# The y products of an AdaLN-conditioned FFN with LoRA experts: two 64-row products per batch pair in place of one block-diagonal product of 128 rows

## The chip, the cores and the metric

The kernel runs on one core of a Trainium2 chip. The metric is the device time of one execution in microseconds (us), as the median of several runs; lower is better. TensorE does the matrix products, ScalarE (ACT), VectorE (DVE) and GpSimd (POOL) copy, split and sum, and SyncE (SP) issues nearly all DMAs.

## The reference, cut to what matters

```python
y = einsum('bct,bcd->bdt', x, W[cond])                 # per batch b: a 64 x 64 matrix, x[b] is 64 x 1024
base = einsum('bsi,oi->bso', y, W_org)                 # 1024 x 1024 projection
q = einsum('bi,ki->bk', y.mean(axis=1), Wq)
coeffs = softmax(einsum('bk,ek->be', q, lora_keys) / sqrt(128))
h = einsum('bsi,eir->bser', y, lora_down)              # 8 experts of rank 64, so 512 columns
out = x + base + einsum('be,bser,ero->bso', coeffs, h, lora_up)
```

There are 64 batches of 64 rows and 1024 columns, all in fp32. The change touches only the first line, which makes y.

## The kernel before

**Tiles.** Two batches make a tile: `x_sb[:, i, :]` has the 64 rows c of batch 0 on partitions 0 to 63 and those of batch 1 on 64 to 127, 1024 columns each. There are 32 tiles, t = 0 to 31, and four tiles make a group q, of which there are 8. x is the stationary operand (what is loaded into TensorE's array), 128 columns at a time, and `cws` is the moving one: a 128 x 128 block diagonal of the two batches' 64 x 64 matrices, copied out of `table` into a buffer whose off-diagonal blocks are set to zero once. One matmul thus gives 128 columns of x by (batch, d) for both batches. A tile takes 8 such matmuls, in two halves n = 2t and 2t + 1 of 4 matmuls each (`make_y(n)`); a half fills one PSUM bank of 512 fp32 columns. An fp32 matmul of the program shows in the trace as two weight loads and two matmuls, so a tile's y is 16 of each. The matmuls of the rest take operands of type fp32r and show as one load and one matmul each.

**After y.** ScalarE copies each half to `y_full` (`copy_y`), from which it is stored to DRAM and summed for the gate, and y is split for the products that follow into a high and a low part, `yq_h` and `yq_l` (`split_y`). Of the first four tiles the even halves are split straight from PSUM, ScalarE making the high part and VectorE the low part and the copy. `make_h(q, a, r)` multiplies the split y of a group by `down` (three passes of high and low parts); then come the LoRA `up` products, and after 380 us the base projection (line 1473), which makes no y.

**Order.** All orders are written out by hand, engine by engine, with semaphores between them. On TensorE a group is: `make_h` quarter, y of one tile of the next group, `make_h` quarter, y of the next tile, and so on four times, then the `up` products. Six of the first eight halves (0, 1, 2, 4, 6, 3; the table `FIRST`) come before the first `make_h`, number 5 within it and number 7 behind it. Twelve matmuls on zeros (line 1520) and the transposition of the LoRA keys (line 1523) stand at the very start; `make_gate` (line 1407) multiplies the keys by `Wq` once. `y_ps`, `h_ps`, `x_ps` and `w_ps` are pairs of PSUM banks. In the steady state the halves of y take turns between the two banks of `y_ps`, and half n waits until half n - 2 has been copied out (`copied(n - 2)`). `y_done` counts finished halves.

Of the kernel before, what the change touches and what calls it, by code (L numbers as in the profile page):

```python
# [26 lines left out]
def adaln_ffn(  # L27
# [51 lines left out]
    with ExitStack() as ctx:  # L79
# [201 lines left out]

        FIRST = (0, 1, 2, 4, 6, 3, 5, 7)
        BY_DVE = (0, 2, 4, 6)
        BY_ACT = (1, 3, 5, 7)

        BEFORE = {6: 0, 3: 1, 5: 2, 7: 4, 8: 6, 9: 3}

        def made(n):
            return FIRST.index(n) + 1 if n < 8 else n + 1

        def tile_made(t):
            return max(made(2 * t), made(2 * t + 1))

# [232 lines left out]
        def _(pool):  # L526
# [10 lines left out]
            def turn_cw(t, rows):  # L537

                if t >= 3:
                    pool.wait_ge(y_done, tile_made(t - 3))  # L540
                for b in range(BT):

                    pool.wait_ge(cw_ready, cw_count(t) + b)
                    pool.tensor_copy(cws[b * C:(b + 1) * C, t % 3, b:b + 1, :, :], table_of(rows[b])).then_inc(cw_ready, 1)  # L544

# [23 lines left out]
            rows_1 = rows_of(1)  # L569
            pool.wait_ge(first_steps, 4)  # L570
            pool.wait_ge(table_loaded, 16)
# [31 lines left out]
        def _(act):  # L603
            def copy(dst, src, done):
                nc.scalar.activation(dst, src, ACT.Copy).then_inc(done, 1)  # L605
# [5 lines left out]
            def turn_cw(t, rows):  # L611
                for b in range(BT):
                    copy(cws[b * C:(b + 1) * C, t % 3, b:b + 1, :, :], table_of(rows[b]), cw_by_act)

            def copy_y(n):
                t, r = n // 2, n % 2
                act.wait_ge(y_done, made(n))
                if n >= 8:

                    act.wait_ge(y_summed, max(n - 7, 8))  # L620
                    act.wait_ge(y_lo[r], t - 3)
                    act.wait_ge(y_stored[n % 8], 16 * (n // 8))
                copy(y_full[:, n % 8, :, :], y_bank(n).rearrange("p (k n) -> p k n", k=4), y_copied)

            def split_y(n):
                t, r = n // 2, n % 2
                i = t % 4
                if n in BY_DVE:

                    act.wait_ge(y_done, made(n))  # L630
                    copy(yq[0][:, 0:4, i * P:(i + 1) * P], y_bank(n).rearrange("p (k n) -> p k n", k=4), y_hi[0])
# [88 lines left out]
            act.dma_start(keys_sb[:, :], lora_keys).then_inc(keys_loaded, 16)  # L720
            act.wait_ge(first_steps, 4)

# [5 lines left out]
            turn_cw(2, rows_2)  # L728
            split_y(0)

            act.wait_ge(y_done, tile_made(0))
            turn_cw(3, rows_3)
            copy_y(1)
            split_y(2)
            split_y(4)
            split_y(6)
            split_down_half(0, 0)
            split_down_half(1, 0)
            split_y(1)
            copy_y(3)  # L740
            split_y(3)
            copy_y(5)
            split_down_half(0, 1)
            split_down_half(1, 1)
            split_y(5)
            copy_y(7)
            split_y(7)
# [126 lines left out]
        def _(dve):  # L874
# [6 lines left out]
            def copy_y(n):  # L881

                dve.wait_ge(y_hi[0], BY_DVE.index(n) + 1)
                nc.vector.tensor_copy(y_full[:, n % 8, :, :],
                                      y_bank(n).rearrange("p (k n) -> p k n", k=4)).then_inc(y_copied_dve, 1)

# [9 lines left out]
            def split_y(n):  # L896
                t, r = n // 2, n % 2
                i = t % 4
                dve.wait_ge(y_hi[r], t + 1)
                if n in BY_DVE:  # L900

                    sub(yq[1][:, 0:4, i * P:(i + 1) * P], y_bank(n).rearrange("p (k n) -> p k n", k=4),
                        yq[0][:, 0:4, i * P:(i + 1) * P], y_lo[0])
# [244 lines left out]
            copy_y(0)  # L1148
            split_y(2)
            split_y(4)  # L1150
            split_y(6)
            split_down_half(0, 0)
            copy_y(2)
            split_down_half(1, 0)
            copy_y(4)
            copy_y(6)
# [180 lines left out]
        def _(pe):  # L1337
            def make_y(n):
                t, r = n // 2, n % 2
                i = t % 4  # L1340
                pe.wait_ge(x_loaded[i], 16 * (t // 4 + 1))
                if n == 1:
# [14 lines left out]
                mm.then_inc(y_done, 1)  # L1357

            def make_h(q, a, r):

                bank = (x_ps, h_ps)[a]
                pe.wait_ge(y_hi[r], 4 * q + 4)
                if q > 0 or a > 0 or r > 0:
                    pe.wait_ge(y_lo[r], 4 * q + 4)
# [5 lines left out]
                for m in range(2):  # L1370
# [10 lines left out]
                    if q == 0 and a == 0 and r == 0 and m == 0:  # L1381

                        for i, (s, w) in enumerate(PASSES):
                            if i == 1:
                                pe.wait_ge(y_lo[0], 4)
                            elif i == 2:
                                pe.wait_ge(down_lo[0], 1)
                            for k in range(4):
                                nc.tensor.matmul(bank[:, m, :], down[w][:, k, col:col + P], yq[s][:, k, :],
                                                 start=(k == 0 and i == 0), stop=False, skip_group_check=True)  # L1390
                        make_y(5)
                        continue
# [10 lines left out]
            def make_gate():  # L1403
                pe.wait_ge(keys_ready, 1)
                pe.wait_ge(wq_loaded, 16)
                for k in range(KC):
# [112 lines left out]
            for n in range(12):  # L1519
                nc.tensor.matmul(w_ps[:, 0, 0:P], gs[:, 0, 0, :], gs[:, 0, 0, :], start=True, stop=True)  # L1520
            pe.wait_ge(first_steps, 4)
            pe.wait_ge(keys_loaded, 16)
            nc.tensor.transpose(keys_ps, keys_sb[:, :], ident[0:E, 0:E]).then_inc(keys_turned, 1)
            for n in FIRST[:6]:
                make_y(n)
            for q in range(NQ):
# [3 lines left out]
                for a in range(2):  # L1530
                    for r in range(2):
                        m = 2 * a + r
                        make_h(q, a, r)
                        if m == 0 and q == 0:
                            make_y(7)
                            make_gate()
                        if m == 1:
                            make_scores(q)
                        if more:
                            make_y(n + 2 * m)  # L1540
                            make_y(n + 2 * m + 1)
                up_1(j0)
# [53 lines left out]
```

## Time and profile before

| | before |
|---|---|
| median of 3 runs | 710.55 us (710.32 to 710.64) |
| the profiled execution | 710.81 us, span of its instructions 709.0 us |
| TensorE matmul busy | 700.6 us (99%) |
| TensorE weight loads busy | 587.1 us (83%) |
| VectorE / ScalarE / GpSimd busy | 504.0 / 287.4 / 127.0 us |

The span runs from the first to the last instruction; 1.8 us of the execution's time lie outside it. Weight loads (PEld) are a row of their own, since they overlap the matmuls (PE). A matmul's duration runs to when its last result is out, so that matmuls that follow closely overlap in the records; what a series of them costs is read from the starts.

### The profile page before, as it was taken

The page shows a single profiled execution, that of the slowest core. Times are in us where ns is not written, and L with a number is a line of the kernel's source. Part 1 is how long each engine was busy: PE and PEld are TensorE (multiplying, and loading weights), DVE is VectorE, ACT ScalarE, POOL GpSimd, SP SyncE. Part 2 cuts the span into 40 slices and gives each one's busy share as a digit, 9 for nine tenths or more (in the row PEclk, how much of TensorE's full clock was granted, in tenths as well). Part 3 has the DMA queues.
Part 4 walks back from the last instruction along what each step waited for, and adds up shares of the span by engine and source line. Part 5 has one row for each costly group of instructions (what it writes and reads, how often), then busy time and mean ns, then how long its engine had stood idle before and what let it go on. Part 6 is the DMA issues. An engine that isn't in the chain of part 4 may idle for free.

```text
span 709.0 us, 10597 instructions
## 1 busy us (share of the span) xinstructions
PE 700.6 (99%) x3345; PEld 587.1 (83%) x3345; DVE 504.0 (71%) x821; ACT 287.4 (41%) x584; POOL 127.0 (18%) x136
## 2 busy tenths in 40 slices
PE   8999999999999999999999999999999999999997
PEld 7887878888888888888888878888888888888876
DVE  4998596685765874655756997668767677776774
ACT  4566666855757642532624722222112222221220
POOL 3310000100100000000000043232332333323360
PEclk9999999999999999999999999999999999999999
DMA  8993393673853934432444836666667776766732
GB/s 240 317 347 125 101 307 137 189 227 128 248 189 120 281 120 120 137 129 62 149 149 146 337 122 188 218 217 217 223 215 238 237 238 223 237 206 213 272 113 89
DMA packets 97049, 137.80 MB, mean 194 GB/s; under 512 B 14810, under 2 KB 66018, under 8 KB 94178
## 3 DMA queue, kind: packets, MB, share of 16 engines
q1 hardware_dynamic: 96976, 137.12, 59.6%
q8 instruction: 27, 0.44, 0.2%
q14 instruction: 28, 0.23, 0.1%
q10 hardware_dynamic: 18, 0.00, 0.0%
HBM read 81.53 MB, written 55.57 MB: 193 GB/s over the span
## 4 chain that ended last, share of the span: by engine, by line
PE 83%; DVE 7%; issue 4%; DMA 2%; SPq 2%; ACT 2%; DVEq 0%; ACTq 0%
PE x_ps L1473 23%; PE w_ps L1473 17%; PE x_ps L1429 11%; PE h_ps L1395 9%; PE x_ps L1395 9%; PE w_ps L1429 8%; PE y_ps L1354 5%; DMA up_raw<-in_L_ffn_lora_up_dram 1%; DMA x_sb<-in_x_dram 1%; SPq L340 1%; DVE ysum L892 1%; DVE tu_l L876 1%; DVE tb_l L876 1%; ACT st L605 1%; DVE blk L879 1%
## 5 line engine op out<-in xcount | busy, mean ns | idle before, releaser
L558 POOL TENSOR_TENSOR blk<-blk,blkx 128x512 f32<-128x512 f32 x60 | 94.1, 1570 | 274.9 <-DVE blk L879 204.7
L879 DVE TENSOR_TENSOR blk<-w_ps,blk 128x512 f32<-128x512 f32 x96 | 66.1, 688 | 67.0 <-PE w_ps L1429 31.0
L1473 PE MATMUL x_ps<-tb_h,ba_h 128*128 128x512 f32 x256 | 100.0, 391 | 0.8 <-DVE ba_l L876 0.4
L1473 PE MATMUL x_ps<-tb_l,ba_h 128*128 128x512 f32 x256 | 99.6, 389 | 0.0
L1473 PE MATMUL x_ps<-tb_h,ba_l 128*128 128x512 f32 x256 | 99.6, 389 | 0.0
L605 ACT ACTIVATE ba_h<-bs 128x512 fp32r<-128x512 f32 x64 | 38.1, 625 | 124.6 <-DVE bs L876 124.6
L1473 PE MATMUL w_ps<-tb_h,ba_h 128*128 128x512 f32 x192 | 74.9, 390 | 0.0
L1473 PE MATMUL w_ps<-tb_l,ba_h 128*128 128x512 f32 x192 | 74.7, 389 | 0.0
L1473 PE MATMUL w_ps<-tb_h,ba_l 128*128 128x512 f32 x192 | 74.7, 389 | 0.0
L544 POOL COPY cws<-table 64x64 f32 x60 | 20.3, 338 | 287.1 <-PE y_ps L1354 274.9
L605 ACT ACTIVATE ba_h<-yb 128x512 fp32r<-128x512 f32 x48 | 28.4, 621 | 103.1 <-DMA yb<-y_dram 103.1
L879 DVE TENSOR_TENSOR blk<-x_ps,blk 128x512 f32<-128x512 f32 x64 | 42.5, 683 | 34.3 <-PE x_ps L1473 34.3
L605 ACT ACTIVATE st<-wt 32x256 f32<-32x256 f32 x128 | 53.1, 415 | 19.4 <-DVE wt L1055 16.5
L1354 PEld LDWEIGHTS y_ps<-cws,x_sb 128*128 128x128 f32 x480 | 57.4, 191 | 3.1 <-issue 0.9
L1354 PE MATMUL y_ps<-cws,x_sb 128*128 128x128 f32 x480 | 59.0, 276 | 0.8 <-ACT y_full L605 0.4
L892 DVE TENSOR_REDUCE ysum<-y_full 128x8 f32<-128x512 f32 x64 | 40.8, 678 | 26.4 <-ACT y_full L605 26.4
L605 ACT ACTIVATE blk<-x_ps 128x512 f32<-128x512 f32 x64 | 38.3, 598 | 51.8 <-PE x_ps L1429 49.7
L876 DVE TENSOR_TENSOR ba_l<-bs,ba_h 128x512 fp32r<-128x512 f32 x64 | 59.2, 944 | 0.0
L1473 PEld LDWEIGHTS x_ps<-tb_h,ba_h 128*128 128x128 f32 x256 | 48.0, 188 | 12.2 <-issue 1.3
L1473 PEld LDWEIGHTS x_ps<-tb_l,ba_h 128*128 128x128 f32 x256 | 48.0, 188 | 10.0
L1473 PEld LDWEIGHTS x_ps<-tb_h,ba_l 128*128 128x128 f32 x256 | 48.1, 188 | 9.9
L1395 PE MATMUL h_ps<-yq_h,down_h 128*128 128x512 f32 x128 | 51.1, 399 | 0.0
(103 smaller groups left out, 1406.2 us busy)
## 6 DMA issues: line engine op xcount, KB each, us to landing
y_dram<-y_full SPq DMA_DIRECT2D x64, 256.0 KB, 3.7
yb<-y_dram SPq DMA_DIRECT2D x32, 512.0 KB, 7.2
out_dram<-blk SPq DMA_DIRECT2D x64, 256.0 KB, 3.9
x_sb<-in_x_dram SPq DMA_DIRECT2D x31, 512.0 KB, 5.3
blkx<-in_x_dram SPq DMA_DIRECT2D x30, 512.0 KB, 7.0
r_dram<-blk SPq DMA_DIRECT2D x56, 256.0 KB, 2.4
blk<-r_dram SPq DMA_DIRECT2D x14, 1024.0 KB, 6.6
t_dram<-st SPq DMA_DIRECT2D x16, 448.0 KB, 5.2
```

Source lines behind the costliest of these rows:

```text
L340: sp.dma_start(raw_piece(n).rearrange("p a k r -> p (a k) r"), down_v[n]).then_inc(down_loaded[n], 16)
L544: pool.tensor_copy(cws[b * C:(b + 1) * C, t % 3, b:b + 1, :, :], table_of(rows[b])).then_inc(cw_ready, 1)
L558: pool.tensor_tensor(blk[p % 3][:, b, :], blk[p % 3][:, b, :], blkx[:, h, n, :], ALU.add).then_inc(x_added, 1)
L605: nc.scalar.activation(dst, src, ACT.Copy).then_inc(done, 1)
L876: nc.vector.tensor_tensor(dst, a, b, ALU.subtract).then_inc(done, 1)
L879: nc.vector.tensor_tensor(dst, a, b, ALU.add).then_inc(done, 1)
L892: nc.vector.tensor_reduce(ysum[:, 4 * r:4 * r + 4, BT * (t % 4):BT * (t % 4) + BT], y_full[:, n % 8, :, :].rearrange("p k (b d) -> p k b d ...
L1354: mm = nc.tensor.matmul(y_bank(n)[:, k * P:(k + 1) * P], x_sb[:, i, col:col + P], cws[:, t % 3, :, :, :].rearrange("p b h d -> p (b h d)") ...
L1395: mm = nc.tensor.matmul(bank[:, m, :], down[w][:, k, col:col + P], yq[s][:, k, :], start=(k == 0 and i == 0), stop=(k == KC - 1 and i == 2 ...
L1429: mm = nc.tensor.matmul(bank, ga[s][:, n, e, :], tu[w][:, n, e, :], start=(first and e == 0 and i == 0), stop=(e == 1 and i == 2), skip_gr ...
L1473: mm = nc.tensor.matmul(bank, ba[s][n][:, k, :], tb[w][n][:, k, :], start=(first and k == 0 and i == 0), stop=(k == 3 and i == 2), skip_gr ...
```

## The change

Each batch of a tile now has matmuls of its own: 64 rows of x are loaded (partitions 0 to 63 for batch 0, 64 to 127 for batch 1) and 64 columns of that batch's own 64 x 64 matrix are streamed. A tile is 16 matmuls of the program instead of 8, in the order k = 0 batch 0, k = 0 batch 1, k = 1 batch 0 and so on. Batch b writes bank b of a pair of banks, so a tile fills a pair, and a half n (k 0 to 3 or 4 to 7) lies in both banks. `cws` has no zero blocks any more, so it is half as wide and its memset is gone. The first three tiles lie in `y_ps`, `w_ps`, `h_ps`, then `y_ps`, `w_ps`, and from tile 5 on all in `y_ps`; a tile waits until both halves of the tile before it in its banks are copied out. All four tiles of the first group are made before the first `make_h`. Since ScalarE and VectorE now read the same banks, waits keep their copies apart in the first four tiles.

```diff
-        cws = small("cws", [P, 3, BT, 2, C // 2])
+        cws = small("cws", [P, 3, 2, C // 2])
-        keys_ps = h_ps[:, 0, 0:E]
+        keys_ps = x_ps[:, 0, 0:E]
...
-        def y_bank(n):
-
-            if n < 8:
-                return (y_ps, w_ps)[n in (2, 4, 5, 7)][:, n not in (0, 6, 2, 5), :]
-            return y_ps[:, n % 2, :]
+        def y_banks(t):
+
+            return (y_ps, w_ps, h_ps, y_ps, w_ps)[t] if t < 5 else y_ps
+
+        def tile_before(t):
+
+            return t - 3 if t < 5 else (t - 2 if t < 6 else t - 1)
+
+        def y_half(n):
+
+            t, r = n // 2, n % 2
+            return y_banks(t)[:, :, 4 * r * C:4 * (r + 1) * C].rearrange("p b (k d) -> p b k d", d=C)
...
-            pool.memset(cws[:, :, :, :, :], 0.0).then_inc(first_steps, 1)
...
             def copy_y(n):
                 t, r = n // 2, n % 2
-                act.wait_ge(y_done, made(n))
+                act.wait_ge(y_done, tile_made(t))
...
-                copy(y_full[:, n % 8, :, :], y_bank(n).rearrange("p (k n) -> p k n", k=4), y_copied)
+                if n == BY_ACT[-1]:
+
+                    act.wait_ge(y_copied_dve, len(BY_DVE))
+                copy(by_batch(y_full[:, n % 8, :, :]), y_half(n), y_copied)
...
-            def make_y(n):
-                t, r = n // 2, n % 2
+            def make_y(t):
...
-                if n in BEFORE:
-                    pe.wait_ge(*copied(BEFORE[n]))
-                elif n >= 10:
-                    pe.wait_ge(*copied(n - 2))
-                for k in range(4):
-                    col = (4 * r + k) * P
-                    mm = nc.tensor.matmul(y_bank(n)[:, k * P:(k + 1) * P], x_sb[:, i, col:col + P],
-                                          cws[:, t % 3, :, :, :].rearrange("p b h d -> p (b h d)"),
-                                          start=True, stop=True)
-                mm.then_inc(y_done, 1)
+                if t >= 3:
+                    for r in range(2):
+                        pe.wait_ge(*copied(2 * tile_before(t) + r))
+                for k in range(KC):
+                    for b in range(BT):
+                        rows64 = slice(b * C, (b + 1) * C)
+                        mm = nc.tensor.matmul(y_banks(t)[:, b, k * C:(k + 1) * C], x_sb[rows64, i, k * P:(k + 1) * P],
+                                              cws[rows64, t % 3, :, :].rearrange("p h d -> p (h d)"),
+                                              start=True, stop=True)
+                        if k == KC - 1:
+                            mm.then_inc(y_done, 1)
```

This is TensorE's program from its first y product to its first h product, of before (`x3` behind a row is three more of the same; `128x128` is the output):

```order
L1354 MATMUL y_ps<-cws,x_sb 128x128 [waits cw_ready,x_loaded_0]
L1354 MATMUL y_ps<-cws,x_sb 128x128 x3
L1354 MATMUL y_ps<-cws,x_sb 128x128 [waits cw_ready,x_rest_loaded,x_loaded_0]
L1354 MATMUL y_ps<-cws,x_sb 128x128 x3
L1354 MATMUL w_ps<-cws,x_sb 128x128 [waits cw_ready,x_loaded_1]
L1354 MATMUL w_ps<-cws,x_sb 128x128 x3
L1354 MATMUL w_ps<-cws,x_sb 128x128 [waits cw_by_act,x_loaded_2]
L1354 MATMUL w_ps<-cws,x_sb 128x128 x3
L1354 MATMUL y_ps<-cws,x_sb 128x128 [waits y_copied_dve,cw_by_act,x_loaded_3]
L1354 MATMUL y_ps<-cws,x_sb 128x128 x3
L1354 MATMUL y_ps<-cws,x_sb 128x128 [waits y_copied,cw_ready,x_loaded_1]
L1354 MATMUL y_ps<-cws,x_sb 128x128 x3
```

And the same stretch of the changed kernel:

```order
L1365 MATMUL y_ps<-cws,x_sb 128x64 [waits cw_ready,x_rest_loaded,x_loaded_0]
L1365 MATMUL y_ps<-cws,x_sb 128x64 x15
L1365 MATMUL w_ps<-cws,x_sb 128x64 [waits cw_ready,x_loaded_1]
L1365 MATMUL w_ps<-cws,x_sb 128x64 x15
L1365 MATMUL h_ps<-cws,x_sb 128x64 [waits cw_by_act,x_loaded_2]
L1365 MATMUL h_ps<-cws,x_sb 128x64 x15
L1365 MATMUL y_ps<-cws,x_sb 128x64 [waits y_copied_dve,y_copied,cw_by_act,x_loaded_3]
L1365 MATMUL y_ps<-cws,x_sb 128x64 x15
L1408 MATMUL x_ps<-yq_h,down_h 128x512 [waits c12_ready,down_hi,keys_ready,y_hi_0]
```

Six half tiles of 4 matmuls became four whole tiles of 16 smaller ones; the halves that stood within and behind the first h products are among them.

Further on, a tile between two h quarters, TensorE before:

```order
L1354 MATMUL y_ps<-cws,x_sb 128x128 [waits y_copied,cw_ready,x_loaded_2]
L1354 MATMUL y_ps<-cws,x_sb 128x128 x3
L1354 MATMUL y_ps<-cws,x_sb 128x128 [waits y_copied,cw_ready,x_loaded_2]
L1354 MATMUL y_ps<-cws,x_sb 128x128 x3
```

and in the changed kernel (two rows of tile 6, then the `up` products behind tile 7):

```order
L1365 MATMUL y_ps<-cws,x_sb 128x64 [waits y_copied,cw_ready,x_loaded_2]
L1365 MATMUL y_ps<-cws,x_sb 128x64 x15
...
L1365 MATMUL y_ps<-cws,x_sb 128x64 [waits y_copied,cw_ready,x_loaded_3]
L1365 MATMUL y_ps<-cws,x_sb 128x64 x15
L1450 MATMUL x_ps<-tu_h,ga_h 128x512 [waits tu_hi,tu_lo,ga_lo_0,ga_hi_0]
```

The place in the order is the same; the number of matmuls doubles, and the one wait covers both halves of the tile before.

## Rows read from the trace of the kernel before

**Rows 1.** Page: busy us, share of the span, instructions of each engine; granted TensorE clock.

```profile
PE 700.6 (99%) x3345; PEld 587.1 (83%) x3345; DVE 504.0 (71%) x821; ACT 287.4 (41%) x584; POOL 127.0 (18%) x136
...
PEclk9999999999999999999999999999999999999999
```

**Rows 2.** Page: the chain of work that ended last, by engine.

```profile
PE 83%; DVE 7%; issue 4%; DMA 2%; SPq 2%; ACT 2%; DVEq 0%; ACTq 0%
```

**Rows 3.** Busy us by stage, instructions in brackets, granted clock, DMA share, GB/s.

```profile
0.00:34.00 34.00, 31.82 (x194) 28.66 (x195) 23.10 (x39) 15.65 (x29) 12.64 (x26) 1.00 0.96 275
34.00:380.00 346.00, 344.24 (x1728) 291.66 (x1727) 236.88 (x464) 190.68 (x417) 14.37 (x46) 1.00 0.53 169
380.00:709.00 329.00, 324.55 (x1426) 266.74 (x1424) 244.04 (x320) 81.02 (x139) 99.98 (x64) 1.00 0.64 213
```

**Rows 4.** The same stages, the y products (line 1354) alone.

```profile
0.00:34.00 34.00, 12.53 (x96) 11.48 (x96) 1.00 0.96 275
34.00:380.00 346.00, 50.91 (x416) 49.95 (x416) 1.00 0.53 169
```

**Rows 5.** Waits of TensorE, 34 to 380 us: us in total, times, longest.

```profile
PE w_ps L1429 <- DVE ga_l L876: 1.0, 1, 1.0
PE y_ps L1354 <- ACT y_full L605: 0.4, 1, 0.4
```

**Rows 6.** Timeline of TensorE around a tile's y: start us, us, work.

```profile
225.67 0.22 PE L1418 MATMUL h_ps<-zs,ones_r 128*128 128x128 f32 x1
225.73 2.00 PE L1354 MATMUL y_ps<-cws,x_sb 128*128 128x128 f32 x16
227.48 0.48 PE L1395 MATMUL h_ps<-yq_h,down_h 128*128 128x512 f32 x1
```

**Rows 7.** Timeline of TensorE's weight loads, same stretch.

```profile
225.67 1.86 PEld L1354 LDWEIGHTS y_ps<-cws,x_sb 128*128 128x128 f32 x16
227.45 0.19 PEld L1395 LDWEIGHTS h_ps<-yq_h,down_h 128*128 128x128 f32 x1
```

**Rows 8.** Lines 1407 and 1523: duration ns min/median/max, first and last start us.

```profile
L1407 PEld LDWEIGHTS h_ps<-keys_t,wq_raw x16: 192/192/192, 21.2 to 22.8; 128*128 128x128 f32 x16
L1407 PE MATMUL h_ps<-keys_t,wq_raw x16: 175/256/256, 21.3 to 22.9; 128*128 128x8 f32 x16
...
L1523 PEld LDWEIGHTS h_ps<-ident,keys_sb x1: 135/135/135, 6.2 to 6.2; 8*128 8x128 f32 x1
```


**Rows 9.** Timeline of weight loads, 5.8 to 6.75 us.

```profile
5.49 0.55 PEld L1520 LDWEIGHTS w_ps<-gs 128*128 128x128 f32 x3
6.16 0.14 PEld L1523 LDWEIGHTS h_ps<-ident,keys_sb 8*128 8x128 f32 x1
6.59 0.30 PEld L1354 LDWEIGHTS y_ps<-cws,x_sb 128*128 128x128 f32 x2 [0.30 <-issue]
```

**Rows 10.** Timeline of weight loads at the gate products.

```profile
21.16 1.87 PEld L1407 LDWEIGHTS h_ps<-keys_t,wq_raw 128*128 128x128 f32 x16
22.94 1.87 PEld L1354 LDWEIGHTS y_ps<-cws,x_sb 128*128 128x128 f32 x16
```

**Rows 11.** Timeline of ScalarE and of TensorE around 80 us.

```profile
79.31 1.08 ACT L605 ACTIVATE y_full<-y_ps 128x512 f32<-128x512 f32 x2
...
80.05 2.02 PE L1354 MATMUL y_ps<-cws,x_sb 128*128 128x128 f32 x16 [0.35 <-ACT y_full L605]
```

**Rows 12.** Timeline of TensorE, start of the program.

```profile
11.45 2.05 PE L1354 MATMUL y_ps<-cws,x_sb 128*128 128x128 f32 x16 [0.20 <-DMA x_sb<-in_x_dram]
13.91 1.17 PE L1389 MATMUL x_ps<-yq_h,down_h 128*128 128x512 f32 x4 [0.40 <-ACT down_h L605]
...
16.75 1.05 PE L1354 MATMUL w_ps<-cws,x_sb 128*128 128x128 f32 x8
```

**Rows 13.** Timeline of GpSimd, start of the program.

```profile
0.73 0.42 POOL L561 MEMSET cws<- 128x384 f32 x1 [0.29 <-POOLq L1585]
...
5.85 0.23 POOL L544 COPY cws<-table 64x64 f32 x1 [4.02 <-DMA table<-in_L_cond_weights_dram]
```

More of the change, by code:

```diff
@@ L278, in b_sum @@
             return bs[n][:, :, :].rearrange("p k (a d) -> p k a d", a=4)
-        FIRST = (0, 1, 2, 4, 6, 3, 5, 7)
         BY_DVE = (0, 2, 4, 6)
         BY_ACT = (1, 3, 5, 7)
-        BEFORE = {6: 0, 3: 1, 5: 2, 7: 4, 8: 6, 9: 3}
-        def made(n):
-            return FIRST.index(n) + 1 if n < 8 else n + 1
         def tile_made(t):
-            return max(made(2 * t), made(2 * t + 1))
+            return 2 * t + 2
         def cw_count(t):
@@ L306, in copied, with by_batch @@
             return y_copied, BY_ACT.index(n) + 1
-        def y_bank(n):
-            if n < 8:
-                return (y_ps, w_ps)[n in (2, 4, 5, 7)][:, n not in (0, 6, 2, 5), :]
-            return y_ps[:, n % 2, :]
+        def y_banks(t):
[5 more added lines that the diff above has]
+            return y_banks(t)[:, :, 4 * r * C:4 * (r + 1) * C].rearrange("p b (k d) -> p b k d", d=C)
+        def by_batch(half):
+            return half.rearrange("p k (b d) -> p b k d", b=BT)
         def down_half(s, n, r):
@@ L543, in turn_cw @@
                     pool.wait_ge(cw_ready, cw_count(t) + b)
-                    pool.tensor_copy(cws[b * C:(b + 1) * C, t % 3, b:b + 1, :, :], table_of(rows[b])).then_inc(cw_ready, 1)
+                    pool.tensor_copy(cws[b * C:(b + 1) * C, t % 3:t % 3 + 1, :, :], table_of(rows[b])).then_inc(cw_ready, 1)
             def add_xz(b):
@@ L569, in _ @@
             rows_1 = rows_of(1)
-            pool.wait_ge(first_steps, 4)
+            pool.wait_ge(first_steps, 3)
             pool.wait_ge(table_loaded, 16)
@@ L612, in turn_cw @@
                 for b in range(BT):
-                    copy(cws[b * C:(b + 1) * C, t % 3, b:b + 1, :, :], table_of(rows[b]), cw_by_act)
+                    copy(cws[b * C:(b + 1) * C, t % 3:t % 3 + 1, :, :], table_of(rows[b]), cw_by_act)
             def copy_y(n):
                 t, r = n // 2, n % 2
-                act.wait_ge(y_done, made(n))
+                act.wait_ge(y_done, tile_made(t))
                 if n >= 8:
@@ L628, in split_y @@
                 if n in BY_DVE:
-                    act.wait_ge(y_done, made(n))
-                    copy(yq[0][:, 0:4, i * P:(i + 1) * P], y_bank(n).rearrange("p (k n) -> p k n", k=4), y_hi[0])
+                    act.wait_ge(y_done, tile_made(t))
+                    copy(by_batch(yq[0][:, 0:4, i * P:(i + 1) * P]), y_half(n), y_hi[0])
                     return
@@ L720, in _ @@
             act.dma_start(keys_sb[:, :], lora_keys).then_inc(keys_loaded, 16)
-            act.wait_ge(first_steps, 4)
+            act.wait_ge(first_steps, 3)
             copy(sexp[:, 0, :], ident[:, 0:E], act_ready)
@@ L729, in _ @@
             split_y(0)
-            act.wait_ge(y_done, tile_made(0))
+            copy_y(1)
             turn_cw(3, rows_3)
-            copy_y(1)
             split_y(2)
+            copy_y(3)
             split_y(4)
+            copy_y(5)
             split_y(6)
@@ L739, in _ @@
             split_y(1)
-            copy_y(3)
             split_y(3)
-            copy_y(5)
+            copy_y(7)
             split_down_half(0, 1)
@@ L745, in _ @@
             split_y(5)
-            copy_y(7)
             split_y(7)
@@ L883, in copy_y @@
                 dve.wait_ge(y_hi[0], BY_DVE.index(n) + 1)
-                nc.vector.tensor_copy(y_full[:, n % 8, :, :],
-                                      y_bank(n).rearrange("p (k n) -> p k n", k=4)).then_inc(y_copied_dve, 1)
+                if n < BY_DVE[-1]:
+                    dve.wait_ge(*copied(n + 1))
+                nc.vector.tensor_copy(by_batch(y_full[:, n % 8, :, :]), y_half(n)).then_inc(y_copied_dve, 1)
             def sum_y(n):
@@ L900, in split_y @@
                 if n in BY_DVE:
-                    sub(yq[1][:, 0:4, i * P:(i + 1) * P], y_bank(n).rearrange("p (k n) -> p k n", k=4),
-                        yq[0][:, 0:4, i * P:(i + 1) * P], y_lo[0])
+                    if n < BY_DVE[-1]:
+                        dve.wait_ge(*copied(n + 1))
+                    sub(by_batch(yq[1][:, 0:4, i * P:(i + 1) * P]), y_half(n),
+                        by_batch(yq[0][:, 0:4, i * P:(i + 1) * P]), y_lo[0])
                     return
@@ L1149, in _ @@
             split_y(2)
+            copy_y(2)
             split_y(4)
@@ L1152, in _ @@
             split_down_half(0, 0)
-            copy_y(2)
+            copy_y(4)
             split_down_half(1, 0)
-            copy_y(4)
             copy_y(6)
@@ L1337, in _ @@
         def _(pe):
-            def make_y(n):
-                t, r = n // 2, n % 2
+            def make_y(t):
                 i = t % 4
                 pe.wait_ge(x_loaded[i], 16 * (t // 4 + 1))
-                if n == 1:
+                if t == 0:
                     pe.wait_ge(x_rest_loaded, 16)
@@ L1362, in make_h @@
                 pe.wait_ge(y_hi[r], 4 * q + 4)
+                if q == 0 and a == 0 and r == 0:
+                    pe.wait_ge(keys_ready, 1)
+                if q == 0 and a == 1 and r == 0:
+                    for n in (4, 5):
+                        pe.wait_ge(*copied(n))
                 if q > 0 or a > 0 or r > 0:
@@ L1405, in make_gate @@
                 pe.wait_ge(wq_loaded, 16)
+                for n in (4, 5):
+                    pe.wait_ge(*copied(n))
                 for k in range(KC):
@@ L1520, in _ @@
                 nc.tensor.matmul(w_ps[:, 0, 0:P], gs[:, 0, 0, :], gs[:, 0, 0, :], start=True, stop=True)
-            pe.wait_ge(first_steps, 4)
+            pe.wait_ge(first_steps, 3)
             pe.wait_ge(keys_loaded, 16)
             nc.tensor.transpose(keys_ps, keys_sb[:, :], ident[0:E, 0:E]).then_inc(keys_turned, 1)
-            for n in FIRST[:6]:
-                make_y(n)
+            for t in range(4):
+                make_y(t)
             for q in range(NQ):
@@ L1534, in _ @@
                         if m == 0 and q == 0:
-                            make_y(7)
                             make_gate()
@@ L1539, in _ @@
                         if more:
-                            make_y(n + 2 * m)
-                            make_y(n + 2 * m + 1)
+                            make_y(4 * (q + 1) + m)
                 up_1(j0)
```

1 line of the change is left out of this document (removed).

## The prediction

> **What bounds the kernel now.** The page's first part and the chain of waits say it together: TensorE's matmuls are busy in 700.6 us of 709.0, at the full granted clock all along [rows 1], and 83% of the chain that ended last is TensorE [rows 2]. The stretches tell where y lies: 344.2 of the 346 us between 34 and 380 us are busy, and y is 416 of the 1728 matmul records there, with 96 more before 34 us; behind 380 us, where the base projection runs, there is none [rows 3, 4]. TensorE's waits in that middle stretch come to under 2 us [rows 5]. So whatever a tile's y costs on TensorE, more or less, arrives in the time nearly in full, and what the other engines do matters only where it makes TensorE wait.
>
> What does one tile's y cost, and what in it is the limit? The busy figure (275 ns or so a record) can't say it, since records overlap. The starts can. The weight loads of a tile begin at 225.67 us and the next h load at 227.45 [rows 7]: 1.78 us for 16 loads, 0.111 us each. 32 tiles make 57.0 us. Whether loading or streaming sets the 0.111 is told by the gate products. They load 128 columns too but stream only 8 columns instead of 128, and their 16 loads take from 21.16 to 22.94 us, 0.111 each again [rows 8, 10]. With next to nothing to stream the step is the same, so **y is bound by its weight loads**, and the matmuls lie beside them. This decides the reading of the change: it halves what is streamed, which costs nothing now, and doubles the number of loads.
>
> **The change part by part.**
>
> *The loads.* A tile's 8 program matmuls become 16, so 16 loads become 32, each of 128 columns but 64 rows; 512 loads are added over the 32 tiles. No row has a 64-row load. The bounds are these.
> - If loads of the two batches go one after the other at the price of a full one: 512 x 0.111 = +57.0 us.
> - If a load of batch 1 runs wholly beside one of batch 0, since they fill different rows of the array: each half of the array gets the 16 loads per tile that the whole array gets now, and the sum is 0.
> - If loads overlap and a 64-row load is also cheaper, the sum is negative. The row nearest to it is the keys' load of 8 rows: 135 ns against the gate loads' 192 [rows 8]. The 57 ns less, taken off the step of 0.111, leave 0.054; half the price and full overlap would be 256 x (0.111 - 0.2225) = -28.5 us, counting by the 256 pairs of k and tile, each of which costs two steps, 0.2225, now. I don't take this one, since that row is a transposition, which differs in more than its rows (it shows one load, where fp32 products of the program show two).
>
> Between the ends I take overlap with a lag. A program matmul of fp32 is load, matmul, load, matmul, and then comes the other batch. The second load of a batch needs the first one's place free, a full step later; the first load of the next batch stands behind that batch's second matmul in the queue and can follow about 0.03 us later (a load at 227.45 us, its matmul at 227.48 [rows 6, 7]), and then runs beside it. A round of both batches is so 2 x (0.111 + 0.030) = 0.282 us against 0.2225, +0.060 for each of 256: **+15.3 us**. If the matmul of 64 columns has to be streamed first (half of 0.111, 0.056, as a bound, since 128 columns take no longer than the step), it is 2 x (0.111 + 0.056) = 0.334, or +28.5.
>
> The Trainium skill, page "TensorE: Matmul & The Clock Gate", section "LDWEIGHTS (loading the stationary operand)", gives the time of a load as columns over 1.2 GHz and says that a load of 32 rows takes what one of 128 rows takes. For 128 columns that is an estimate of 107 ns, beside the measured 111; it speaks against this change, for by it no load becomes cheaper, and the best sum is 0. The 135 ns of the 8-row load don't fit it, unless the transposition explains them.
>
> *Going in and out of half-array products.* The keys' matmul is the one place where the rows in use change. Its load starts at 6.16 us; the last load of the zeros before it starts at 5.49 + 0.55 - 0.19 = 5.85 us [rows 8, 9]. That is 0.31 us where 0.111 is usual: 0.20 us more, which may be a wait for the array to empty or for a semaphore. The y of tiles 4 to 31 stand singly between h products and the first four together, so there are 29 stretches. I price the way in at 0.20 (+5.8 us) and leave the way out at nothing, because the matmul before it is short; bounds are 0 and both ways, +11.6 us.
>
> The Trainium skill, page "TensorEngine Tiling (Array Packing)", section "Key Properties", says that changing the tiling mode drains TensorE, and that different tiles can load weights and multiply in parallel. By the first the 5.8 us are real; by the second the overlap is, though whether two loads run together it doesn't say, and no run of this trace shows it.
>
> *Waits.* A tile now waits for both halves of the tile before it, whose second copy used to be wanted only half a tile later. Tile 9 already waits (start at 80.05 us, 0.35 us idle), and ScalarE's two copies run from 79.31 to 80.39 us [rows 11]: +0.4 us, once, since the other waits for y copies don't exist [rows 5]. Behind the waiting y stands only the next h quarter, and a delay there is in the sum already. Copies start up to 0.9 us later, as they want a whole tile; ScalarE is busy in 190.7 of 346 us [rows 3], and the copies that nothing else follows on TensorE for a quarter of h have that as cover; without it each tile would cost up to 0.9 us. That copies read 64-column runs out of two banks instead of one run of 512 I price at nothing under the same cover.
>
> *The start.* Before, six halves are done and the first h product starts at 13.91 us, with y halves put in at 16.75 and later. Now eight halves come first. The last tile of before starts at 11.45 us, held by its DMA [rows 12]; three whole tiles from 6.59 us [rows 9] end at 6.59 + 5.3 = 11.9 at today's price. The first h product comes some 1.8 us later, two halves (1.8 us) are gone from behind it, sum 0 but for the price of y, which is counted above. The memset of `cws` takes 0.42 us from 0.73 us on, and GpSimd then idles 4.02 us for the table [rows 13]; dropping it gives 0.
>
> **Sum.** 710.81 + 15.3 + 5.8 + 0.4 = 732.3 us for the profiled execution. That one lies 0.26 over the median of the runs, so 732 us for the median.
>
> **The rivals.**
> - *Loads in series.* The two batches' loads don't run together, at 0.111 each: 710.5 + 57.0 + 5.8 + 0.4 = 773.7, from 768 without to 780 with both switches. For it: loads follow one another at the same step wherever the trace has several, whatever is streamed. Against it: all of those use the whole array, so they could not overlap. Chance 0.30.
> - *A 64-row load costs half, and loads overlap* (faster than before). For it: 135 ns against 192. From 710.5 - 28.5 + 5.8 = 688 to, with the lag of 0.030, 256 x (2 x (0.054 + 0.030) - 0.2225) = -14, 702. It decides once a round of both batches with its share of the switches (5.8 / 256 = 0.023) is under 0.2225, that is once a load costs less than 0.070 with that lag. Chance 0.22.
> - *Nothing changes*: full overlap, no lag, switches that cost under 1.4 us. Or the loads are half price and in series, with free switches. 710 to 712. Chance 0.08.
>
> **How the numbers follow.** The forecast, overlap with lag, has 0.40; its own range is from 712 (no lag, little for the switches) to 710.5 + 28.5 + 11.6 + 0.4 = 751. The range has to reach to the serial case, or it would leave out 3 in 10, and takes in no change: 700 to 778, which leaves out most of the faster case and the last end of the serial one. Below 0.2% (1.4 us) this kernel's measurement can't tell a change from none. Faster 0.22, no change 0.08, slower 0.40 + 0.30 = 0.70.
>
> **What would show it.** In the changed profile the loads of a tile's y, 32 of them, should take 2.26 us plus the switch from the first to the next h load; 3.6 us means series, 1.8 full overlap, under 1.4 cheaper loads. The gap between the last h load and the first y load shows the switch: 0.2 us more than today's. The chain of waits should remain TensorE's, with no new wait of over 1 us for copies. I am wrong in sign if the y stretch is shorter than 1.78 us, and wrong in mechanism if the time grows by idle time of TensorE on ScalarE's copies.

## The result, and the profile after

The changed kernel takes 724.35 us (median of 4 runs, 721.95 to 728.62) against 710.43 for the kernel before: a ratio of 1.0202, 95% interval 1.0177 to 1.0228. It is slower, by 13.9 us, inside the predicted range and 8 us under the forecast. The profiled execution took 726.1 us. The spread of 6.7 us is itself news, since the kernel before spreads by 1 us in its four runs; it goes with the granted clock: the four runs have 0.987, 0.995, 0.986 and 0.994 for 726.1, 721.95, 728.62 and 722.59 us.

The head of the page, to be read against [rows 1, 2]: TensorE is 99% busy as before, and the chain is now 92% TensorE. What is new is the clock, low in slices 1 and 2 of 40.

```profile
span 724.3 us, 11627 instructions
...
PE 716.1 (99%) x3857; PEld 594.3 (82%) x3857; DVE 504.1 (70%) x821; ACT 285.5 (39%) x584; POOL 121.3 (17%) x135
...
PEclk7799999999999999999999999999999999999999
...
PE 92%; DVE 3%; issue 2%; ACT 1%; DMA 1%; DVEq 0%; POOL 0%; SPq 0%; ACTq 0%; POOLq 0%
```

**The y of a tile.** The weight loads of tile 17, of which [rows 7] show the kernel before:

```profile
237.08 0.19 PEld L1439 LDWEIGHTS h_ps<-zs,ones_r 128*128 128x128 f32 x1
237.45 1.86 PEld L1365 LDWEIGHTS y_ps<-cws,x_sb 64*128 64x128 f32 x32 [0.19 <-issue]
239.38 0.19 PEld L1413 LDWEIGHTS h_ps<-yq_h,down_h 128*128 128x128 f32 x1
```

32 loads take 1.86 us, exactly as long as 16 took. A load of 64 rows is about as long as one of 128:

```profile
L1365 PEld LDWEIGHTS y_ps<-cws,x_sb x928: 182/188/330, 7.1 to 353.3; 64*128 64x128 f32 x186
```

The median is 188 ns, where it was 192 for 128 rows. So the two batches' loads run side by side, and pair follows pair at the old step: (1.86 - 0.19) / 15 = 0.111 us. Next, the same tile's matmuls, for [rows 6]:

```profile
237.30 0.22 PE L1439 MATMUL h_ps<-zs,ones_r 128*128 128x128 f32 x1
237.46 2.00 PE L1365 MATMUL y_ps<-cws,x_sb 64*128 64x64 f32 x32
239.39 0.50 PE L1413 MATMUL h_ps<-yq_h,down_h 128*128 128x512 f32 x1
```

From the start of the scores product (the one on `zs`) to the start of y it was 0.06 us and is 0.16; from y to the next h product it was 1.75 and is 1.93. Together 0.28 us are lost here. How they divide between the way in and the way out depends on whether matmuls or loads are read. These are the loads at the way into tile 16, with the last h load before it, in the kernel before and in the changed one:

```profile
217.98 0.19 PEld L1395 LDWEIGHTS x_ps<-yq_h,down_l 128*128 128x128 f32 x1
218.20 1.98 PEld L1354 LDWEIGHTS y_ps<-cws,x_sb 128*128 128x128 f32 x16
...
229.25 0.19 PEld L1413 LDWEIGHTS x_ps<-yq_h,down_l 128*128 128x128 f32 x1
229.79 1.86 PEld L1365 LDWEIGHTS y_ps<-cws,x_sb 64*128 64x128 f32 x32 [0.35 <-issue]
```

The first y load came 0.22 us after the last h load and now comes 0.54 after it, so by the loads nearly all of the loss lies before the stretch. The loads now stand idle before 27 of the y stretches between 34 and 380 us, 8.8 us in all and for nothing that the profile shows, where it was 0.6 us, once. Only the sum of both sides is certain. Over a whole group of four tiles it is more accurate. These are the y starts of tiles 16 and 20 of the changed kernel,

```profile
229.79 2.00 PE L1365 MATMUL y_ps<-cws,x_sb 64*128 64x64 f32 x32
...
279.29 2.00 PE L1365 MATMUL y_ps<-cws,x_sb 64*128 64x64 f32 x32
```

and of tiles 4, 16 and 20 of the kernel before:

```profile
22.97 2.03 PE L1354 MATMUL y_ps<-cws,x_sb 128*128 128x128 f32 x16
...
218.43 1.95 PE L1354 MATMUL y_ps<-cws,x_sb 128*128 128x128 f32 x16
...
266.56 1.95 PE L1354 MATMUL y_ps<-cws,x_sb 128*128 128x128 f32 x16
```

A group takes 279.29 - 229.79 = 49.50 us against 266.56 - 218.43 = 48.13: 1.37 more for four tiles, **0.34 us a stretch**. For 28 stretches that is 9.6 us.

**The start** (TensorE's timeline, for [rows 12]) has the rest:

```profile
7.14 2.00 PE L1365 MATMUL y_ps<-cws,x_sb 64*128 64x64 f32 x32 [0.65 <-POOL cws L550]
8.94 3.25 PE L1365 MATMUL w_ps<-cws,x_sb 64*128 64x64 f32 x32
11.93 3.68 PE L1365 MATMUL h_ps<-cws,x_sb 64*128 64x64 f32 x32
15.34 3.68 PE L1365 MATMUL y_ps<-cws,x_sb 64*128 64x64 f32 x32
20.32 2.05 PE L1408 MATMUL x_ps<-yq_h,down_h 128*128 128x512 f32 x4 [1.29 <-ACT down_h L610]
...
30.55 2.00 PE L1365 MATMUL w_ps<-cws,x_sb 64*128 64x64 f32 x32
```

From the start of the first tile's y to that of the second it is 1.80 us, then 2.99 and 3.41, the fourth tile's record is as long as the third's, and tile 4 starts its y at 30.55 us, where the kernel before had it at 22.97 (the first row of its y starts above). Busy time by stretch says why (the brackets hold numbers of instructions; the first figure behind the last bracket is the granted clock, 1.00 being 2.4 GHz and 0.50 being 1.2):

```profile
5.00:9.00 4.00, 3.35 (x43) 3.17 (x42) 0.17 (x1) 0.51 (x2) 0.93 (x4) 1.00 1.00 352
9.00:26.00 17.00, 15.71 (x112) 14.30 (x110) 9.59 (x14) 8.44 (x18) 3.43 (x4) 0.51 1.08 252
26.00:34.00 8.00, 8.00 (x67) 7.11 (x66) 7.93 (x12) 2.62 (x6) 4.24 (x6) 0.97 1.04 393
```

And the kernel before, from 9 to 26 us:

```profile
9.00:26.00 17.00, 16.23 (x110) 14.48 (x110) 14.78 (x22) 9.80 (x18) 7.25 (x8) 1.00 1.02 245
```

TensorE is nearly as busy as it was, 15.71 of 17 us against 16.23, but at half clock.

The Trainium skill, page "TensorE: Matmul & The Clock Gate", Part 1, says that the clock is set by how busy the engine has been. By these rows an engine that its records show as busy can still get half the clock, and the runs below show what differs.

TensorE's waits in the middle stretch, for [rows 5]:

```profile
PE y_ps L1365 <- ACT y_full L610: 0.4, 1, 0.4
PE x_ps L1450 <- ACT blk L610: 0.3, 1, 0.3
```

No new wait. The wait for the y copy is as long as it was, and the 1.0 us on `ga_l` is gone, presumably because TensorE now comes later to the product that waited for VectorE. Before 34 us there is a longer wait, 1.3 us for `down_h` where it was 0.4 (the 20.32 row above, against [rows 12]).

### The profile page after: what moved, and what is told of

Read it like the earlier page. It is cut to its first block, busy times and chain, and to the rows that moved or that the text cites. A ratio compares the mean times of both kernels' runs of the same rounds, so it can differ in the third digit from the quotient of the medians.

```text
span 724.3 us, 11627 instructions
## 1 busy us (share of the span) xinstructions
PE 716.1 (99%) x3857; PEld 594.3 (82%) x3857; DVE 504.1 (70%) x821; ACT 285.5 (39%) x584; POOL 121.3 (17%) x135
## 4 chain that ended last, share of the span: by engine, by line
PE 92%; DVE 3%; issue 2%; ACT 1%; DMA 1%; DVEq 0%; POOL 0%; SPq 0%; ACTq 0%; POOLq 0%
PE x_ps L1494 22%; PE w_ps L1494 17%; PE h_ps L1413 12%; PE x_ps L1450 11%; PE x_ps L1413 10%; PE w_ps L1450 8%; PE y_ps L1365 8%; DVE tb_l L883 1%; PE x_ps L1408 1%; PE w_ps L1365 1%; DMA table<-in_L_cond_weights_dram 1%; DVE blk L886 1%; DVE ysum L900 0%; PE h_ps L1365 0%; ACT st L610 0%
## 5 line engine op out<-in xcount | busy, mean ns | idle before, releaser
L550 POOL COPY cws<-table 64x64 f32 x60 | 15.0, 250 | 298.8 <-PE y_ps L1365 279.7
L1365 PEld LDWEIGHTS y_ps<-cws,x_sb 64*128 64x128 f32 x928 | 55.8, 192 | 9.5 <-issue 9.5
L1365 PE MATMUL y_ps<-cws,x_sb 64*128 64x64 f32 x928 | 59.7, 280 | 1.1 <-POOL cws L550 0.6
```

The lines of the kernel that those rows point to most:

```text
L550: pool.tensor_copy(cws[b * C:(b + 1) * C, t % 3:t % 3 + 1, :, :], table_of(rows[b])).then_inc(cw_ready, 1)
L1365: mm = nc.tensor.matmul(y_banks(t)[:, b, k * C:(k + 1) * C], x_sb[rows64, i, k * P:(k + 1) * P], cws[rows64, t % 3, :, :].rearrange("p h d ...
```

## The experiments

All times are medians; each is compared with the kernel before on the same chip (710.41 us in the first four, 709.88 in the next four, 709.58 in the last).

**e1, e2: which part of the change costs what.** In e1 tiles 0 to 3 are made as before, in halves of 128 rows in the old order, and only tiles 4 to 31 by the new products. e2 is the reverse.

In `make_y` of e1, on top of the kernel before:

```diff
+                if n >= 8:
+                    if r == 1:
+                        return
+                    for m in ((6, 3) if n == 8 else (n - 2, n - 1)):
+                        pe.wait_ge(*copied(m))
+                    for k in range(KC):
+                        for b in range(BT):
...
```

In `make_y` of e2, on top of the changed kernel (`cws` and its memset are as before the change):

```diff
+                if t >= 4:
+                    for r in range(2):
+                        pe.wait_ge(*copied(2 * tile_before(t) + r))
+                        for k in range(4):
...
```

> The start of the kernel before (block-diagonal halves for tiles 0 to 3), two-batch products of 64 rows from tile 4 on. Theory 1 (the 14 us are the way in and out of half-array products, 0.28 us for each of 28 stretches, plus a lower granted clock near the program's start): 710.4 + 28 x 0.28 = 718 us, clock 1.00 all along, 7.60 us from one tile's y to the next. Rival (the low clock comes with 64-row products wherever they stand): clock below 0.99 again and 724 us. Rival (the loss is all in the start's new order): 710 to 711 us.

Measured: 720.21 us, ratio 1.0140 (1.0124 to 1.0155). The one run at clock 1.000 took 719.52, the three at 0.997 took 720.17 to 720.34. That is 9.1 us for the 28 stretches at full clock, 0.33 each, with nothing taken off for the 1.0 us on `ga_l`, which is gone here too. I expected 718, having read 0.28 off one tile. The clock was not quite full all along as expected: there is a short low stretch, after the first 64-row tile.

```profile
22.00:25.00 3.00, 3.00 (x42) 2.91 (x42) 2.96 (x7) 1.61 (x2) 1.74 (x2) 1.00 1.12 249
25.00:29.00 4.00, 4.00 (x11) 3.11 (x11) 3.94 (x5) 2.16 (x4) 1.94 (x3) 0.57 1.08 354
29.00:33.00 4.00, 4.00 (x31) 3.31 (x29) 2.25 (x6) 0.01 (x1) 0.70 (x2) 1.00 1.00 389
```

> The reverse: the changed kernel's start with four 64-row tiles, block-diagonal halves from tile 4 on. Theory 1: only the start's loss is left, 710.4 + 6 to 7 = 717 us, with a granted clock of 0.98 to 0.99 over the span and a low stretch within the first 30 us. Rival (the start is late because of its order and its waits, with no help of the clock): 717 us as well, but at clock 1.00. Rival (all loss is in the later stretches): 710 us.

Measured: 711.85 us, ratio 1.0043 (1.0021 to 1.0066), from 12 runs. Nine took 711.0 to 712.4 at clock 0.997 to 1.000, three 716.4 to 718.2 at 0.987 to 0.989. The new order of the start costs about 1 us, and the rest is the clock, in some runs only. Where the 1 us arises, the profiled run at full clock shows. Tile 4's y and the h product behind it, in the kernel before and in e2 (both with 128-row products in this tile):

```profile
22.97 2.03 PE L1354 MATMUL y_ps<-cws,x_sb 128*128 128x128 f32 x16
24.76 0.48 PE L1395 MATMUL x_ps<-yq_h,down_h 128*128 128x512 f32 x1
...
23.63 2.03 PE L1368 MATMUL w_ps<-cws,x_sb 128*128 128x128 f32 x16
26.22 0.47 PE L1427 MATMUL x_ps<-yq_h,down_h 128*128 128x512 f32 x1 [0.56 <-POOL yq_l L536]
```

From y to h it was 1.79 us and is 2.59, 0.80 more: the h product now waits for a low part of y that GpSimd writes. e4 and e5 below have the same wait, of 0.5 and 0.6 us. The profiled run of the changed kernel hasn't got it; there TensorE came later, at the low clock, which is presumably why. The expected 717 us was right for three runs of twelve.

**e3: must the batches take turns?** All eight products of batch 0, then those of batch 1.

```diff
-                for k in range(KC):
-                    for b in range(BT):
+                for b in range(BT):
+                    for k in range(KC):
```

> The changed kernel, but batch 0's eight products of a tile first and then batch 1's. If loads run beside each other only when neighbours in the program fill different halves of the array, a tile's 32 loads take 32 x 0.111 = 3.6 us instead of 1.8, and the time is 724 + 32 x 1.8 = 781 us. If the queue reaches far enough to pair them anyway, 724 us and 1.8 us a tile. In between, if some at the seam are paired.

Measured: 804.96 us, one run, clock 0.940. A tile in a stretch at full clock:

```profile
223.25 3.39 PE L1365 MATMUL y_ps<-cws,x_sb 64*128 64x64 f32 x32
226.56 0.50 PE L1413 MATMUL h_ps<-yq_h,down_h 128*128 128x512 f32 x1
```

From y to the next h product it is 3.31 us where it was 1.93, so most loads are in series. Without turns the pairing is gone but for the seam between the batches: from 224.58 to 224.97 us 9 of these loads are under way, and 4 in the same length at the start of the tile (223.25 to 223.64). This is nearly the rival "loads in series". Over 32 tiles the 1.38 us are 44 us, and 720 + 44 = 764. The remaining 41 us I put down to the low clock, which now came back again and again (0.91 in the mean from 34 to 440 us). That is argued, not shown: by the profiled run of the changed kernel, where a mean clock of 0.987 went with 6.3 us over 719.8, a mean of 0.940 over 803 us would be some 32 us, an estimate, which leaves 9 open.

**e4, e5: what brings the clock down.** The products of tiles 0 to 3 (e4) or of all tiles (e5) stream their 64 columns twice, but for the last k of a tile, which streams them once; the second copy lands where the next k is written and is overwritten by it. Loads, rows in use and order stay. This is e5; in e4 `w` is 2 only where also t < 4.

```diff
+                        w = 2 if k < KC - 1 else 1
-                        mm = nc.tensor.matmul(y_banks(t)[:, b, k * C:(k + 1) * C], x_sb[rows64, i, k * P:(k + 1) * P],
-                                              cws[rows64, t % 3, :, :].rearrange("p h d -> p (h d)"),
+                        mm = nc.tensor.matmul(y_banks(t)[:, b, k * C:(k + w) * C], x_sb[rows64, i, k * P:(k + 1) * P],
+                                              cws[rows64, t % 3, :, :].rearrange("p h d -> p (h d)").unsqueeze(1).to_broadcast([C, w, C]),
```

> The changed kernel, but in tiles 0 to 3 each product streams its 64 columns twice (the second copy is overwritten by the next product), so that 128 columns are streamed for each load, as before the change; loads and order stay. If the granted clock falls because the array streams little between the loads, it now stays at full, and the time is 724 - 6 = 718 us. If it falls because only half the rows are in use, or because of waits between the tiles, the start is as in the changed kernel: 722 to 728 us and clock 0.985 to 0.995.

Measured: 722.16 us, ratio 1.0160 (1.0140 to 1.0181): two runs of 718.9 and 719.3 us at clock 0.999, three of 722.2 to 722.5 at 0.995 to 0.998. No run at 0.985 to 0.989 any more, but the median was not the expected 718, so the question stood half open. The weight loads of the start, at twice the columns:

```profile
6.57 1.86 PEld L1366 LDWEIGHTS y_ps<-cws,x_sb 64*128 64x128 f32 x32
8.35 1.87 PEld L1366 LDWEIGHTS w_ps<-cws,x_sb 64*128 64x128 f32 x32
10.13 1.87 PEld L1366 LDWEIGHTS h_ps<-cws,x_sb 64*128 64x128 f32 x32
11.92 1.87 PEld L1366 LDWEIGHTS y_ps<-cws,x_sb 64*128 64x128 f32 x32
```

Each tile's loads start 1.78 us after the last tile's. Streaming 128 columns is free here, as the gate products had said.

> The changed kernel with every y product streaming its 64 columns twice (in the run before, only those of tiles 0 to 3 did). If the low clock comes from how little the array streams per load, no run falls any more: granted clock 0.999 or 1.000 in each, 719 us in each, spread under 1 us. If it comes from the half-array loads themselves, runs of 722 us and clock 0.995 to 0.998 stay. If streaming had a price of its own, the 1.78 us from one tile's first load to the next in the start would grow; I expect it not to.

Measured: 719.87 us, ratio 1.0140 (1.0125 to 1.0156), four runs from 719.53 to 720.32, each at clock 1.000. The same stretches as above:

```profile
5.00:9.00 4.00, 2.79 (x45) 2.60 (x45) 0.17 (x1) 0.75 (x3) 0.92 (x4) 1.00 0.89 344
9.00:26.00 17.00, 15.15 (x167) 13.57 (x164) 14.51 (x21) 9.82 (x19) 7.21 (x8) 1.00 1.11 259
26.00:34.00 8.00, 8.00 (x60) 6.74 (x60) 7.38 (x16) 3.62 (x7) 3.39 (x6) 1.00 1.06 388
```

Streaming more cost nothing: every run lies within 0.6 us of the changed kernel's fastest (719.78 us, below). The array had the same loads, rows and order, and TensorE was no busier from 9 to 26 us (15.15 us against 15.71); only the columns streamed differ, and with them the clock. Four runs would be few to say so, but the three versions below stream the same way: of the 18 runs of e5, e6, e7 and e9, 17 have a clock of 0.999 or 1.000 and one, of e7, 0.997, where 8 of the changed kernel's 10 runs (here and in e8) have 0.985 to 0.997.

**e8: the changed kernel again**, for its runs beside these.

> The changed kernel itself once more, beside the others on one chip: 722 to 728 us with the granted clock going from 0.995 to 0.986 as the time rises; a run at full clock, if there is one, should take 719 us. If runs of one clock differ by more than 1 us, something other than the clock varies.

Measured: 721.01 us, ratio 1.0144 (1.0128 to 1.0159), six runs, four of them below the expected 722: 719.78 and 719.80 us at clock 0.999, 720.84 at 0.997, 721.18 at 0.994, 726.73 at 0.988, 728.00 at 0.985. Time follows the clock. At full clock the change costs 719.8 - 709.9 = 9.9 us, and the low clock adds up to 8.

**e6: is it the stretch or what is in it?** As e5, with the y of tiles 12 to 31 in two stretches.

```diff
+                    if m == 1 and 2 <= q < NQ - 1:
+                        make_y(4 * (q + 1) + 2 * a + r, range(0, 4))
...
-                            make_y(4 * (q + 1) + m)
+                            make_y(4 * (q + 1) + m, range(4, KC) if q >= 2 else range(KC))
```

> As e5, and the y of tiles 12 to 31 is made in two stretches of four k, one in the middle of an h quarter and one behind it, so 20 more stretches. Theory (each stretch of half-array products between whole-array ones costs 0.34 us, whatever its length): e5 + 6.8 us = 726 us. Rival (the price is that of the products in it, a slower step in a stretch, not of going in and out): no more than e5 + 1 us. A third way, waits for copies that now come too soon, would show as TensorE waiting on y_full.

Measured: 728.16 us, ratio 1.0254 (1.0240 to 1.0268), 8.3 us over e5 with the same number of products. TensorE's timeline:

```profile
223.36 0.39 PE L1416 MATMUL x_ps<-yq_h,down_l 128*128 128x512 f32 x1
223.68 1.16 PE L1366 MATMUL y_ps<-cws,x_sb 64*128 64x128 f32 x16
224.77 0.50 PE L1416 MATMUL x_ps<-yq_h,down_h 128*128 128x512 f32 x1
...
227.40 0.39 PE L1416 MATMUL x_ps<-yq_h,down_l 128*128 128x512 f32 x1
227.72 1.11 PE L1366 MATMUL y_ps<-cws,x_sb 64*128 64x128 f32 x16
228.76 0.50 PE L1416 MATMUL x_ps<-yq_h,down_h 128*128 128x512 f32 x1
```

A stretch of half the length has the same edges: 0.32 us from the last h product, where h follows h at 0.23, and then 0.34 to the second h product. 8.3 / 20 is 0.41 a stretch, more than 0.34, and no wait for copies grew. The rows account for the difference. The stretch of k 0 to 3 takes 1.09 us to the next h product, that of k 4 to 7 takes 1.04: the first ends with products that stream 128 columns, the second with the last k, which streams 64. So each added stretch costs the edges and 0.05 us for a longer last product, some 0.40. That the streamed columns are the reason fits these rows; no run has them changed alone. A stretch of 128-row products has no such price: in the kernel before, 0.22 + 1.71 + 0.31 us from the h product before tile 18's y to the second one behind it are no more than 16 steps of 0.111 and two of 0.23.

**e7, e9: fewer stretches.** As e5, and from tile 8 on two tiles a stretch, the odd ones in `w_ps`.

```diff
+                if t >= 9 and t % 2 == 1:
+                    pe.wait_ge(c11_ready, 2 * (t // 4 - 1))
+                    pe.wait_ge(c21_ready, 2 * (t // 4 - 1))
...
+                        elif more and m % 2 == 0:
+                            make_y(4 * (q + 1) + m)
+                            make_y(4 * (q + 1) + m + 1)
...
                 up_1(j0)
+                if more:
+                    pe.wait_ge(*copied(n + 6))
+                    pe.wait_ge(*copied(n + 7))
```

> As e5, and from tile 8 on two tiles are made in one stretch, the odd ones in w_ps, so 12 stretches fewer (17 for 29). Theory (0.34 us a stretch): e5 - 4.1 us = 715 us, still over the kernel before. Rival (a new wait of the up products for the copies out of w_ps, or of y for w_ps to be free): no gain or a loss, with idle time of TensorE on y_full or blk.

Measured: 721.77 us, ratio 1.0167 (1.0153 to 1.0181), slower than e5. The rival held. TensorE's longest waits, and ScalarE around one of them:

```profile
PE w_ps L1454 <- ACT y_full L610: 4.4, 6, 1.7
```

```profile
193.75 0.60 ACT L610 ACTIVATE y_full<-w_ps 128x512 f32<-128x512 f32 x1
199.77 0.42 ACT L610 ACTIVATE ga_h<-g 128x256 fp32r<-128x256 f32 x1 [5.42 <-DVE g L991]
200.09 0.58 ACT L610 ACTIVATE y_full<-w_ps 128x512 f32<-128x512 f32 x1
```

The group's last half of y has been ready for several us when ScalarE copies it at 200.09: the copy stands behind the high part `ga_h` of block 2, and that waits for VectorE until 199.77. TensorE's first `w_ps` product now needs the copy and starts at 200.77. e9 puts the copy first:

```diff
                     copy_y(n + 6)
+                    copy_y(n + 7)
 
                 hi_block(j0, P2, 0, 1)
-                if more:
-                    copy_y(n + 7)
```

> As e7, with ScalarE's copy of the group's last y half moved ahead of the high part for up_2, behind which it stood waiting for VectorE while TensorE's first w_ps product waited for the copy. Theory (0.34 us a stretch, and e7 lost it again to this one wait of about 1 us in each of six groups): 719.9 - 4.1 = 715.8 us, no wait of w_ps products on y_full, 0.7 us less from group to group than in e5. Rival (pairs of tiles cost something else, in the copies' or the loads' timing): still over 719 us with the wait gone.

Measured: 716.75 us, ratio 1.0098 (1.0081 to 1.0115), the wait gone. Two y starts a group apart:

```profile
222.37 2.00 PE L1368 MATMUL y_ps<-cws,x_sb 64*128 64x128 f32 x32
...
271.20 2.00 PE L1368 MATMUL y_ps<-cws,x_sb 64*128 64x128 f32 x32
```

48.83 us a group, 0.67 less than with single stretches for two stretches fewer, so 0.33 each. Over the whole kernel it is 3.1 us under e5 and not the expected 4.1. Its waits between 34 and 380 us account for the rest: 0.7 us on `ga_l`, which e5 didn't have, and 0.6 on `blk` where e5 had 0.3. It is the best of the versions that make all tiles with 64-row products, and slower than the kernel before by 7 us. None of the runs points to a version that beats that kernel.

## Why the prediction was right, and where it wasn't

The sign and the case (loads overlap, the rest is lost around them) were right; the sizes of the terms mostly were not, and their errors partly cancelled.

- **y is bound by its loads, streaming is free.** Right: twice the columns changed nothing in a tile's 1.78 us (e4). No load got cheaper with 64 rows (188 ns against 192, and 0.111 us a step), so the best this change could do for y was nothing, and the rival with loads at half price falls; the keys' short load in [rows 8] was due to something else, which no run here isolates. The Trainium skill, page "TensorE: Matmul & The Clock Gate", section "LDWEIGHTS (loading the stationary operand)", has the rule that a load goes by its columns and not its rows, and the trace agrees.
- **Overlap with a lag, +15.3 us.** Overlap right, lag wrong: the term is 0. I had the second load of a batch hold up the next batch; in the trace pairs of loads go in step, and a tile's stretch of loads up to the next h load is 1.93 us, not 2.26 and more. What the term did say right is that neighbours decide: with the batches one after the other (e3) a tile takes 1.38 us more.
- **In and out of half-array products, +5.8 us.** Mis-sized: 0.34 us a stretch, 28 stretches, 9.6 us. I priced the way in by the keys' product and left the way out at nothing, "because the matmul before it is short"; neither was right. By the starts of the matmuls at tile 17 the way out has 0.18 us and the way in 0.10; by the starts of the loads at tile 16 nearly all is on the way in. The gap before the first y load, which I wanted 0.2 us longer, is 0.14 longer at tile 17 and 0.31 to 0.32 at tile 16. e6 and e9 show that the price hangs on the number of stretches. The Trainium skill's page "TensorEngine Tiling (Array Packing)", section "Key Properties", says that a change of mode drains TensorE; that something is lost at each change agrees with it, and the rows give the size, but no run shows that it is a drain.
- **Waits, +0.4 us.** The wait stayed what it was, so 0; and a wait of 1.0 us on VectorE was covered by the later TensorE. The sum at full clock is so 9.6, less the 1.0, and about 1 for the start (e2); measured 9.9.
- **The start, 0 us.** Right at full clock up to tile 4, whose y starts at 22.87 us in e4 and at 22.97 before. The h product behind it then waits 0.5 to 0.6 us for GpSimd (e2, e4, e5), which the term left out; it is most of the 1 us that e2 costs. And one step was missing altogether: four tiles in a row of products with few columns per load were followed by 17 us at 1.2 GHz in the profiled run. It costs 0 to 8 us from run to run, some 4 in the median of the result. I had read the clock row and concluded that it stays.

The forecast of 732 lay 8 us from the measured 724 partly by luck: a term of 15 that wasn't there stood against 4 for edges that cost 9.6 and not 5.8, and 4 for a clock that wasn't priced. At full clock, where the changed kernel takes 719.8 us, the forecast is 12 us off.

**Shown and argued.** That streaming 128 columns a load and not 64 keeps the clock up is shown by e5 against e8, with nothing else changed, and borne out by e6, e7 and e9. Why only some runs of one program fall is not settled: e2, e4 and e8 have runs of both kinds. Whether the 0.34 us are the emptying of the array or another cost of changing the rows in use wasn't separated.

## What to carry to other kernels

Before shrinking an operand, find out which of its two sides sets the pace: a few products in the same trace with almost nothing to stream told here that loading did, and so halving the streaming could bring nothing. Half-array products do run in pairs, if neighbours in the program take turns, but each stretch of them between whole-array products costs a third of a us, so they want to be gathered in few long stretches. And a phase that streams less per load may lose the clock while TensorE's busy share stays at 90%: look at the granted clock of each run, and not only of one.

## What the runs showed of the hardware

- Two loads of 64 rows by 128 fp32 columns in different halves of the array run side by side (32 in 1.86 us, as 16 of 128 rows before). With a program order that didn't alternate it was 3.31 us to the next product and not 1.93, with most of the loads in series.
- Going from whole-array products into a stretch of half-array ones and out again cost 0.34 us, for 16 pairs of loads (49.50 against 48.13 us for four) and for 32 alike (e9).
- Streaming 128 columns and not 64 per load, for the same result, left the fastest run as it was (719.5 against 719.8 us) and made the kernel steadier (0.8 against 8.2 us of spread), through the clock.
- The clock fell from 2.4 to 1.2 GHz with TensorE 92% busy by its records (15.71 of 17 us).
